# A two-layer adapter and FFN kernel on one core: four moves in the order of its stages

## What is computed

```
y   = einsum('bct,bcd->bdt', x, L0_cond_weights[itok_B_0_15])      # a 64 x 64 matrix per sequence
h   = relu(layernorm(y @ gw1.T + gb1) * ln_gamma + ln_beta)        # gate, 32 channels
w   = softmax over the top 2 of 8 experts (h @ gw2.T + gb2), zero where an expert has over 768 tokens
x1  = x + y @ W0.T + sum over experts of (y @ lora_A[e] * w[e]) @ lora_B[e] / 16
z   = x1 @ L1_cond_weight[itok_B_3_7].T                            # one of 8 matrices per sequence
deq(m) = round(clip(m / (s + 1e-5), -1, 1)) * s,   s = mean(|m|)   # w_gate, w_up, w_down: 2752 x 1024
out = x1 + ((z @ deq(w_gate).T) * (z @ deq(w_up).T)) @ deq(w_down).T
```

## Time and profile before

| | us |
|---|---|
| median of three runs | 1442.25 (1441.39 to 1443.23) |
| the profiled execution, own time | 1444.66 |
| its span | 1442.7 |
| TensorE busy | 1338.7 (93%) |
| VectorE busy | 727.2 (50%) |
| ScalarE busy | 409.8 (28%) |
| GpSimd busy | 141.8 (10%) |
| granted TensorE clock, mean | 0.983 of full speed |

### The profile page before, as it was taken

How to read it: one execution, slowest core, us unless ns; L and a number is a source line. 1 busy time by engine, 2 the same in 40 slices (tenths; PEclk the granted TensorE clock), 3 DMA queues, 4 the chain that set the end, 5 groups by cost and what they waited for, 6 DMA issues and landing times.

```text
span 1442.7 us, 23467 instructions
## 1 busy us (share of the span) xinstructions
PE 1338.7 (93%) x8864; PEld 853.2 (59%) x8864; DVE 727.2 (50%) x1186; ACT 409.8 (28%) x464; POOL 141.8 (10%) x79
## 2 busy tenths in 40 slices
PE   2597979999999998999999999999999999999998
PEld 1464645545454444544444488874688854888843
DVE  1446456433635333788876255565255573455521
ACT  0355555111112133777762011120011120111100
POOL 3200000000000000000000012220022210122200
PEclk9999989999999999999999999999999999999999
DMA  9389999559792823999967554445643454643354
GB/s 251 92 327 404 378 398 347 117 123 284 212 202 88 195 70 101 316 330 330 332 206 266 177 176 149 153 156 190 228 149 145 149 208 141 238 146 143 140 192 139
DMA packets 172525, 302.47 MB, mean 210 GB/s; under 512 B 99073, under 2 KB 131073, under 8 KB 164641
## 3 DMA queue, kind: packets, MB, share of 16 engines
q1 hardware_dynamic: 151616, 265.11, 55.7%
q10 hardware_dynamic: 19808, 35.79, 7.2%
q0 software_dynamic: 1024, 0.53, 0.2%
HBM read 212.39 MB, written 68.03 MB: 194 GB/s over the span
## 4 chain that ended last, share of the span: by engine, by line
PE 64%; DVE 10%; DMA 9%; ACT 6%; issue 6%; ACTq 3%; SPq 1%; POOL 1%; POOLq 0%; DVEq 0%
PE pair L931 25%; PE pair L968 15%; PE pair L821 11%; PE pair L739 5%; ACTq L1052 2%; DMA wb_scratch<-region_q 2%; DMA region_w<-in_L_ffn_w_up 2%; PE pair L895 2%; DMA region_q<-wb_scratch 2%; DMA region_w<-in_L_ffn_w_gate 2%; PE pair L654 2%; ACT region_q L1143 2%; PE pair L757 1%; PE pair L707 1%; DVE region_q L1566 1%
## 5 line engine op out<-in xcount | busy, mean ns | idle before, releaser
L931 PE MATMUL pair<-act_t,region_q 128*128 128x256 f16 x3696 | 404.0, 273 | 0.0
L931 PEld LDWEIGHTS pair<-act_t,region_q 128*128 128x128 f16 x3696 | 361.6, 98 | 42.5 <-DMA region_q<-wa_scratch 0.2
L968 PE MATMUL pair<-region_q,region_w 128*128 128x512 f16 x1232 | 269.4, 381 | 5.5 <-DMA region_q<-wb_scratch 5.2
L639 POOL TENSOR_TENSOR region_w<-region_q,region_w 128x1792 f32 (+1 forms) x33 | 118.4, 3587 | 1202.7 <-ACT region_w L1168 1202.7
L968 PEld LDWEIGHTS pair<-region_q,region_w 128*128 128x128 f16 x1232 | 120.4, 98 | 153.2 <-DMA region_q<-wb_scratch 7.1
L821 PE MATMUL pair<-region_w,act_t 128*128 x816 | 186.1, 385 | 5.2 <-issue 3.6
L739 PE MATMUL pair<-region_w,act_t 128*128 128x512 f16 x768 | 169.2, 380 | 0.0
L895 PE MATMUL pair<-act_t,region_q 128*128 128x512 f16 x704 | 157.9, 383 | 3.7 <-issue 3.7
L1263 DVE SCALAR_TENSOR_TENSOR act_t<-pair,act_t 128x512 f32 (+1 forms) x66 | 61.0, 946 | 168.2 <-ACT act_t L1002 168.2
L821 PEld LDWEIGHTS pair<-region_w,act_t 128*128 x816 | 81.0, 99 | 98.8 <-issue 12.3
L1174 ACT ACTIVATE region_q<-pair 128x512 f32<-128x512 f32 x33 | 19.7, 597 | 403.3 <-PE pair L931 403.3
(11 more groups left out here) (182 smaller groups left out, 1033.4 us busy)
## 6 DMA issues: line engine op xcount, KB each, us to landing
region_q<-wa_scratch SPq DMA_DIRECT2D x33, 1792.0 KB, 7.3
region_q<-wb_scratch SPq DMA_DIRECT2D x28, 1408.0 KB, 6.1
region_q<-in_L_cond_weight SPq DMA_DIRECT2D x40, 512.0 KB, 12.2
w1s_scratch<-region_q ACTq DMA_DIRECT2D x40, 512.0 KB, 8.7
wa_scratch<-region_q SPq DMA_DIRECT2D x22, 896.0 KB, 5.7
region_w<-in_L_ffn_w_gate SPq DMA_DIRECT2D x16, 688.0 KB, 12.9
region_w<-in_L_ffn_w_up SPq DMA_DIRECT2D x16, 688.0 KB, 13.8
wb_scratch<-region_q SPq DMA_DIRECT2D x11, 896.0 KB, 4.1
```

The costliest lines, as they stand in the source:

```text
L639: pool.tensor_tensor(at(iop[:, 1], u), st[s][:, 0:7], at(iop[:, 0], u), ALU.subtract)\
L931: mm = pe.matmul(bank(s_bank, b)[:, (1 - h) * HALF:(2 - h) * HALF], ring_a[s][:, h, o_a, k], moving[a], start=(opens and h == 1 and k == 0 ...
L968: mm = pe.matmul(bank(s_bank, b), iop[:, a, p, o_a, tp * P:(tp + 1) * P], ring_b[r][:, p], start=(opens and p == 0 and a == 0), stop=(not ...
```

## The change

1. **A factors on SyncE's queue.** The eight loads of `lora_a` leave ScalarE's program and stand in SyncE's, behind the sixth x tile and ahead of the first `load_w`.
2. **Gating of a quarter over three steps.** `quarter_top` is cut into `quarter_prod` and `quarter_top`; for quarters 0 to 2 `quarter_mean`, `quarter_prod` and `quarter_top` stand behind `w_step` in steps m, m + 1 and m + 2, and ScalarE's `gate_root` behind `w_step` of step m + 1. Quarter 3 stays whole in step 13.
3. **Sums of up and down in the linear stage.** The condition stage sums `w_gate` alone, 16 pieces, one a step in steps 1 to 10 and two a step in 11 to 13. `w_up` (ScalarE, `sum_up`) and `w_down` (VectorE, `sum_down`) are summed in 12 pieces each of 1835 columns, in turn in the same six buffers, at the *start* of slots 0, 1, 2, 3, 5 and 9, ahead of the slot's split of x1. SyncE loads pieces 0 to 3 behind the first pair of transposing loads, 4 to 11 behind the second, 12 to 17 behind the third; ScalarE issues 18 to 23 in slot 6. The reductions stand in slot 9.
4. **First group product ahead of the last transposes.** `gate_up(0, 0)` moves ahead of `linear_t(16)`, with its gate half in `pair[1]`; `scale_gate(0, 0)` and `product(0, 0, 0, 0)` move ahead of the last split of z.

The core of the diff; left out are the declarations of tiles and semaphores and the changed names:

```diff
-NPIECE = 12
-PIECE = -(-INNER * D // P // NPIECE)
+NPIECE = 24
+PIECE = -(-2 * INNER * D // P // NPIECE)
...
-SUMS_AT = {m: tuple(range(3 * m - 3, min(3 * m, 32))) for m in range(1, 12)}
+SUMS_AT = {**{m: (m - 1,) for m in range(1, 11)}, 11: (10, 11), 12: (12, 13), 13: (14, 15)}
 LAST_TURN = 12
 CHUNK_AT = 9
-PIECES_AT = {3: (0, 1, 2), 4: (3, 4, 5), 7: (6, 7, 8), 8: (9, 10, 11)}
+PIECES_AT = {0: range(0, 4), 1: range(4, 6), 2: range(6, 10), 3: range(10, 12), 5: range(12, 18), 9: range(18, 24)}
+LATE_PIECES_AT = 6
...
+
+        def gate_bank(n, s):
+
+            return pair[1][:, H:D] if isinstance(n, int) and n == 0 else pair[0][:, s * H:(s + 1) * H]
...
+        def load_piece(eng, p):
+            at_p, n = piece_cols(p)
+            if p >= NSD:
+                eng.wait_ge((up_summed, down_summed)[p % 2], (p - NSD) // 2 + 1)
+            eng.dma_start(stat_in[p % NSD][:, 0:n], (up_flat, down_flat)[p % 2][:, at_p:at_p + n])\
+               .then_inc(piece_loaded[p % NSD], 16)
...
@@ -484,6 +499,9 @@
                 if m == 0:
                     for t in range(3, NXR):
                         load_x(t)
+                    for k in range(KC):
+                        sp.dma_start(lora_a_nat[:, k], lora_a[:, k * P:(k + 1) * P, :].rearrange("e i r -> i e r"))\
+                          .then_inc(lora_loaded, 16)
...
-            sp.wait_ge(gate_summed, 2 * NPIECE_G)
+            sp.wait_ge(gate_summed, NPIECE_G)
...
+            for p in range(4):
+                load_piece(sp, p)
...
-                if r in (1, 2):
-                    for p in range(NSD * r - NSD, NSD * r):
-                        load_piece(p)
+                    for p in range(4, 12):
+                        load_piece(sp, p)
+                if r == 2:
+                    for p in range(12, 18):
+                        load_piece(sp, p)
...
+            def gate_up(n, s):
...
+                if isinstance(n, int) and n == 0:
+                    pe.wait_ge(z_copied_a, FIRST_OPTIONAL - 1)
+                    pe.wait_ge(z_copied_v, FIRST_OPTIONAL - 1)
+                if isinstance(n, int) and n == 1:
+                    pe.wait_ge(gate_scaled, 1)
+                for dst, first in ((gate_bank(n, s), 2), (pair[1][:, s * H:(s + 1) * H], 0)):
...
+                                           start=(k == 0 and a == 0), stop=(k == KC - 1 and a == 1))
+                mm.then_inc(gu_done, 1)
...
-            pe.wait_ge(stat_summed, 2)
+            pe.wait_ge(stat_summed, 3)
...
             linear_t(k - 2, 1)
+            pe.wait_ge(z_low, GRP // SEQ)
+            gate_up(0, 0)
             linear_t(k - 1, 0)
             pairs = field(pe, F_CUM, NADP - 1, NSLOT)
             for n in range(k, NSLOT):
                 with pe.If(pairs > n):
+                    if n == k:
+                        pe.wait_ge(prod_done, 1)
...
-            pe.wait_ge(z_low, GRP // SEQ)
-            gate_up(0, 0)
             pe.wait_ge(slots_done, 1)
             turn_q(2, 0, 1)
             gate_up(1, 1)
...
-            for k in range(KC):
-                act.dma_start(lora_a_nat[:, k], lora_a[:, k * P:(k + 1) * P, :].rearrange("e i r -> i e r"))\
-                   .then_inc(lora_loaded, 16)
             act.dma_start(lora_b_nat, lora_b.rearrange("e r o -> (e r) o")).then_inc(lora_loaded, 16)
...
-                if m in QUARTER_AT:
-                    gate_root(QUARTER_AT[m])
                 if m == NT - 3:
+                    gate_root(3)
...
+                if m - 1 in QUARTER_AT and m - 1 != NT - 3:
+                    gate_root(QUARTER_AT[m - 1])
                 for p in SUMS_AT.get(m, ()):
                     sum_gate(p)
...
+            def sum_up(p):
+                at_p, n = piece_cols(p)
+                act.wait_ge(piece_loaded[p % NSD], piece_count(p))
+                act.activation(stat_in[p % NSD][:, 0:n], stat_in[p % NSD][:, 0:n], ACT.Abs,
+                               accum_out=stat_u[:, p // 2:p // 2 + 1]).then_inc(up_summed, 1)
+
             for k in range(LAST_TURN + 1):
+                for p in PIECES_AT.get(k, ())[::2]:
+                    sum_up(p)
                 for t in TURNS[k]:
                     x1_part(t)
...
+                if k == LATE_PIECES_AT:
+                    for p in range(18, NPIECE):
+                        load_piece(act, p)
                 if k == CHUNK_AT:
-                    act.wait_ge(stat_done, NPIECE)
+                    act.wait_ge(up_summed, NPIECE // 2)
+                    act.wait_ge(down_summed, NPIECE // 2)
                     load_q(act, 0, 0, 0)
...
+            scale_gate(0, 0)
             high_z(k - 1)
...
-                scale_gate(m - 1, (m - 1) % 2)
+                if m > 1:
+                    scale_gate(m - 1, (m - 1) % 2)
...
+                else:
+                    v.wait_ge(quarter_step, (QT + 1) * j)
...
-            def quarter_top(j):
+            def quarter_prod(j):
...
+
+            def quarter_top(j):
+                own = slice(j * QT, (j + 1) * QT)
                 v.wait_ge(quarter_step, (QT + 1) * j + QT)
...
-                if m in QUARTER_AT:
-                    quarter_mean(QUARTER_AT[m])
-                    if m == NT - 3:
-                        quarter_top(QUARTER_AT[m])
-                        gate_weights()
+                if m == NT - 3:
+                    quarter_mean(3)
+                    quarter_prod(3)
+                    quarter_top(3)
+                    gate_weights()
...
-                if m in QUARTER_AT and m != NT - 3:
-                    quarter_top(QUARTER_AT[m])
+                for q, part in enumerate((quarter_mean, quarter_prod, quarter_top)):
+                    if m - q in QUARTER_AT and m - q != NT - 3:
+                        part(QUARTER_AT[m - q])
...
-            v.wait_ge(gate_summed, 2 * NPIECE_G)
-            v.tensor_reduce(ssum[:, 0:2], stat_g[:, :, :], X, ALU.add).then_inc(stat_summed, 1)
+            v.wait_ge(gate_summed, NPIECE_G)
+            v.tensor_reduce(ssum[:, 0:1], stat_g[:, :], X, ALU.add).then_inc(stat_summed, 1)
...
-            def sum_piece(p):
...
+            def sum_down(p):
+                at_p, n = piece_cols(p)
+                v.wait_ge(piece_loaded[p % NSD], piece_count(p))
+                v.tensor_reduce(stat_d[:, p // 2:p // 2 + 1], stat_in[p % NSD][:, 0:n], X, ALU.add,
+                                apply_absolute_value=True).then_inc(down_summed, 1)
 
             for k in range(LAST_TURN + 1):
+                for p in PIECES_AT.get(k, ())[1::2]:
+                    sum_down(p)
...
-                for p in PIECES_AT.get(k, ()):
-                    sum_piece(p)
-            v.wait_ge(stat_done, NPIECE)
-            v.tensor_reduce(ssum[:, 2:3], stat[:, :], X, ALU.add).then_inc(stat_summed, 1)
+                if k == max(PIECES_AT):
+                    v.wait_ge(up_summed, NPIECE // 2)
+                    v.wait_ge(down_summed, NPIECE // 2)
+                    v.tensor_reduce(ssum[:, 1:2], stat_u[:, :], X, ALU.add).then_inc(stat_summed, 1)
+                    v.tensor_reduce(ssum[:, 2:3], stat_d[:, :], X, ALU.add).then_inc(stat_summed, 1)
...
+            product(0, 0, 0, 0)
             low_z(k - 1)
```

More of the change, by code:

```diff
@@ L399, in load_q, with piece_cols, piece_count @@
                                   wd_view[:, :, ds((p + h * NP - 1) * P + P, cols)]).then_inc(wq_loaded[4 + h], 16)
+        gate_flat, up_flat, down_flat = [w.rearrange("a b -> (a b)").rearrange("(p n) -> p n", p=P)
+                                         for w in (w_gate, w_up, w_down)]
+        def piece_cols(p):
+            return p // 2 * PIECE, min(PIECE, INNER * D // P - p // 2 * PIECE)
+        def load_piece(eng, p):
[4 more added lines that the diff above has]
+               .then_inc(piece_loaded[p % NSD], 16)
+        def piece_count(p):
+            return 16 * (gate_pieces(p % NSD) + p // NSD + 1)
         def store_wa(eng, p, h, n):
@@ L423, in gate_pieces @@
         def gate_pieces(s):
-            return len(range(s, 2 * NPIECE_G, NSG)) if s < NSG else 0
+            return len(range(s, NPIECE_G, NSG)) if s < NSG else 0
         def x1_stores(i):
@@ L450, in load_w @@
                     sp.dma_start(w_nat[q], w1_rows[ds(row_i + (4 * (j % 2) + q) * P, P), :]).then_inc(w_loaded[q], 16)
-            flat = [w.rearrange("a b -> (a b)").rearrange("(p n) -> p n", p=P) for w in (w_gate, w_up, w_down)]
             def load_sum(p):
                 s = p % NSG
-                at_p = p % NPIECE_G * PIECE_G
                 if p < NSG:
@@ L861, in turn_q @@
                     mm.then_inc(q_turned[kind], 1)
+            def gate_up(n, s):
+                pe.wait_ge(q_out[0], n + 1)
+                pe.wait_ge(q_out[1], n + 1)
+                wait_if(pe, prod_done, n - 1)
+                if isinstance(n, int) and n == 0:
[4 more added lines that the diff above has]
+                for dst, first in ((gate_bank(n, s), 2), (pair[1][:, s * H:(s + 1) * H], 0)):
```

(24 more changed lines are left out.)

27 lines of the change are left out of this document (8 added, 19 removed).

## The result

The changed kernel took 1389.32 us (median of four runs, 1387.45 to 1393.39) against 1441.82 for the kernel before beside it; the ratio is 0.9646, 95% interval 0.9613 to 0.9678. With five more runs of it that I made later (`after_again`), its nine runs have the median 1390.5 and lie between 1386.3 and 1397.5. The profiled execution took 1390.51 us (span 1388.9); the prediction's sum for it was 1388.9.

A forecast was written before the change was run, and what follows sets the result against it. The prediction took TensorE, busy 93% of the span, as the bound, with only idle and slow stretches to win. Its terms -29, -18.7, -8.1 and 0 sum to -55.8 us, forecasting 1386.4 us, range 1376 to 1406.

The forecast's parts named there:

- A factors, -29: Start: with the factor loads off ScalarE's queue, the first mix comes at 26 us instead of 55.2.
- R1: Start: the A factors land late on SyncE's queue, gain only 9 to 15 us, 1400 to 1406 us; chance 0.09.
- R5: Start: gains only its issue time, 4 us instead of 29, 1411 us; chance 0.01.
- Condition stage, -18.7: Condition stage: 17.0 us of waits and 3.7 of slow clock go, less 2 us allowed for late transfers.
- R3: Condition stage: becomes transfer-bound, losing 13 us instead of the 2 allowed, 1397 us; chance 0.10.
- Gate sums later, 0: Ahead of the linear stage: later gate sums delay the first transposing loads, covered by 6.5 us of slack, costing 0.
- Linear stage, -8.1: Linear stage: removed waits and their slow clock give -15.1 us, late pieces 4 and 5 in step 1 cost +7.
- 5 us to spare: Linear stage, step 5: pieces 12 to 17 come behind the third transposing pair with this slack, so no wait.
- R2: Linear stage: waits for pieces, step 1 losing 17 us instead of 7, step 5 about 10; 1396 to 1410; chance 0.14.
- First group product, 0: Passage to group products: product fills both gaps, but a later 6.4 us idle takes the gain back; bounds -2 and +2.
- R4: Linear stage: transposing loads collapse to 50 GB/s, 84 us a pair, kernel slower at 1566 us; chance 0.03.
- R6: Whole kernel: no effect, as TensorE's early start is lost at a later barrier; chance 0.01.

The follow-up runs named there:

- factors_back: The changed kernel with the eight A factor loads on ScalarE's queue again; 1424.43 us.
- sums_back: The changed kernel with three w_gate and w_up sums a step in the condition stage again, linear stage summing w_down alone in 12 pieces; 1410.58 us.
- first_six: The changed kernel with pieces 0 to 5 issued ahead of the second transposing pair, 12 to 17 summed in slot 6, 18 to 23 issued in slot 7; 1379.26 us.
- product_back: The changed kernel with the first group product, its scaling and gate_up(0, 0) behind the last transposes again; 1390.96 us.
- load_first: The changed kernel with pieces 0 to 5 issued ahead of the second transposing pair and slot 2's four sums moved to slot 3; 1390.82 us.

## Why the prediction was right, step by step

The forecast of 1386.4 stands 2.9 us below the median; the sum on the profiled clock, 1388.9, against 1390.5. Of the 53.8 us by which the span shrank, 29.5 lie before the first mix, 19.3 in the condition stage and 4.7 in the linear stage; the passage gives 1.0 back and the rest wins 1.3. The two larger sums so hold within 1 us, in part by luck: 3.0 us less from part 1 are covered by 3.6 us more from parts 2 and 3. The linear stage came out at little more than half of its sum, and in the other profiled execution at none of it.

**A factors, -29.** The first mix moved by 29.5 us. But of this 3.0 are lost before gate(0) starts: `factors_back` needs 14.0 us from the second mix to gate(0), the changed kernel 17.0 (30.15 to 47.14), 1.2 of it the wait for the factors, the rest mostly a lower clock (3.24 and 11.00 us for what takes 2.02 and 10.52). So the part is worth 27. The factors came later than I put them, the queue free at 40.3 instead of landing at 38, since they held SyncE for 15.02 us, not 6.2; the cover held but for 1.2 us. By the prediction's own signs a wait of gate(0) for the factors speaks against it; it came, but small. R1 and R5 fall. The Trainium skill (DMA: Bandwidth & Descriptors, "Issuing engines are not separate DMA queues") calls the time to initiate a transfer usually small beside the transfer. Here it was not small: the same eight loads held ScalarE for 34.73 us and SyncE for 15.02, and moving them won 27.

**Condition stage, -18.7.** Measured -19.3 with those 3.0 us inside, so the waits, the clock and the transfers together gave -22.3 (`factors_back` against before), more than the bound of -20.7 for waits and clock: the 2 us allowed for late transfers were not needed. The round trip of 0.9 us that was to stay is 0.80. R3, a stage bound by transfers, falls: TensorE is idle for 0.45 us in 54, and the same stretch of `sums_back` moves more bytes. The windows (us, busy, clock, DMA share, GB/s), the changed kernel first, then `sums_back`:

```profile
112.00:166.00 54.00, 53.55 (x345) 1.00 0.98 372
```

```profile
112.00:166.00 54.00, 54.00 (x340) 0.97 1.01 402
```

The Trainium skill (DMA: Bandwidth & Descriptors, "Where 436 GB/s comes from") gives about 358 GB/s as a core's HBM limit; both windows are above it.

**Gate sums later, 0.** The first linear product waits for no load.

**Linear stage, -8.1.** Measured: -4.7 in one execution and +1.7 in the other that was profiled. This is the step that failed, in two terms. The wait in slot 1 was foreseen in its place and mechanism, but at 5.2 and 1.8 us; it measured 9.05 and about 1.6 (0.9 + 0.7 over full-clock times), because the second pair took 26.95 us where I had 22. With that the sum is -4.5 instead of -8.1, which is the first execution. And slot 5 did not have "5 us to spare": the last piece landed 0.8 us ahead of its use in the first profile and was late by 1.7 in the other. The prediction's two times for it, 388.5 and 386, give 5 us only if the 7 us lost in slot 1 are added to the second, and no row gives the 388.5. The gain of 15.1 us for the waits removed was about right: `first_six`, with only small waits in their place, has 14.4. R2 was the true danger: it put 10 us on the forecast in slot 1 and 10 in slot 5, and the linear stage came out 3.4 us above its sum in one execution and 9.8 in the other.

**First group product, 0.** Measured +1.0, of which 0.6 stand in `product_back` too, without this part. The idle 6.4 us are 6.92, and the second product lost 0.6 us to the clock, not 1.9.

**R4 and R6** fall: no transposing pair takes over 36 us in any profiled run (27.0 at most in the changed kernel), and nothing later swallows the gain; the rest is 849.6 us against 850.9.

## What to carry to other kernels

When a wait is won at one place in a stage fed by one load queue, look at once for the next consumer of that queue: the end of the transfers doesn't move, and the wait reappears there, so that two half-right edits can each measure as nothing and only their sum as 11 us. Place each load by its deadline, ahead of a long one with a later deadline, and ask for it a slot after it has landed, not in the slot in which it lands. A total that doesn't answer to an edit is no verdict on its theory until the same instruction has been timed in both traces.

## What was unexpected in the hardware

The third transposing pair did not end sooner for being issued sooner. Issued at 311 us, 15 us behind the last piece ahead of it, it took 19.64 us (22.03 in `after_again`); issued at 299, 1.6 to 8.3 us behind the last piece, it took 30.64 to 35.88 in four kernels. It ended at 330.7, 333.7 and between 330.1 and 335.3. The DMA engines were full all this time, in the middle stretch at half the bytes of its neighbours, here in `load_first` (last columns DMA share and GB/s):

```profile
296.00:311.00 15.00, 15.00 (x80) 1.00 1.09 347
311.00:332.00 21.00, 18.88 (x101) 1.00 1.22 180
332.00:345.00 13.00, 12.93 (x66) 1.00 1.08 361
```

And the time that an engine is held by issuing the same eight loads of 64-byte runs was 34.73 us on ScalarE's queue beside other loads (35.27 in `factors_back`) and 15.02 on SyncE's queue behind them. The queue and its company changed together; no run tells which of the two it was.
